# Four node stages of a graph network with their 25 blocks written out, and one combined weight for three vector axes

## The reference

```python
h = relu(layernorm(x))
# layer 0, before its 103125 edges: two node-wise maps, scaled by the node's number z
s0, s1 = (h_s @ W_sc0) * z / 8, einsum('nuc,uw->nwc', h_v, W_sc1) * z / sqrt(32)
h0, h1 = (h_s @ W_l1_0) * z / 8, einsum('nuc,uw->nwc', h_v, W_l1_1) * z / sqrt(32)
# edges: gather h0, h1 at the source, weight by an MLP of the edge, sum at the target: ns (n,96), nv (n,96,3)
# layer 0's end
x = x + concat(sin * s0 + cos * (ns @ W_l2_0) * z / sqrt(96),
               sin * s1 + cos * einsum('nuc,uw->nwc', nv, W_l2_1) * z / sqrt(96))
# layer 2 needs h with features down the partitions; layer 3 maps the normed h twice, and its sums once
```

## Time and profile before

| | |
|---|---|
| median of 3 runs | 11916.89 us (11911.71 to 11928.06) |
| profiled execution, its own time | 11895.75 us |
| its span | 11893.6 us |
| TensorE busy | 8785.1 us, 74% |
| VectorE busy | 8795.3 us, 74% |
| GpSimd busy | 7695.5 us, 65% |
| ScalarE busy | 4487.7 us, 38% |

### The profile page before, as it was taken

One profiled execution on the slowest core, in us unless ns is written; L12 is line 12 of the kernel. 1 busy time (PEld: TensorE's weight loads), 2 busy tenths in 40 slices (PEclk: granted clock), 3 DMA queues, 4 the chain that ended last, 5 costly groups with the idle time before them and its releaser, 6 DMA issues. The chain is left out here.

```text
span 11893.6 us, 249543 instructions
## 1 busy us (share of the span) xinstructions
PE 8785.1 (74%) x62786; PEld 6128.9 (52%) x62787; DVE 8795.3 (74%) x26209; ACT 4487.7 (38%) x15002; POOL 7695.5 (65%) x12520
## 2 busy tenths in 40 slices
PE   4655555199995676666677767588888888888887
PEld 2111111067774444444444433277777777777776
DVE  8977777378884444443555569588999889999997
ACT  0000000056662111111222200177767777776775
POOL 1777777657774777772677700077777777777775
PEclk9777777589996888886899989699999999999998
DMA  4111111023332333331333367100000000000000
GB/s 138 28 28 31 28 28 27 13 62 77 77 77 49 76 76 76 76 76 34 91 91 90 85 116 140 24 22 21 22 21 21 21 21 21 21 22 21 21 22 21
DMA packets 901065, 597.78 MB, mean 50 GB/s; under 512 B 654029, under 2 KB 831011, under 8 KB 898312
## 3 DMA queue, kind: packets, MB, share of 16 engines
q0 software_dynamic: 235616, 359.73, 12.0%
q1 hardware_dynamic: 650440, 197.82, 9.2%
q10 hardware_dynamic: 14624, 35.51, 0.8%
HBM read 512.98 MB, written 79.56 MB: 50 GB/s over the span
## 5 line engine op out<-in xcount | busy, mean ns | idle before, releaser
L1278 POOL DMA_INDIRECT l1s_node_rows<-node_table,l1s_edge_rows x1216 | 1310.6, 1078 | 467.0 <-issue 366.4
L1624 POOL DMA_INDIRECT l2s_node_rows<-node_table,l2s_edge_rows x864 | 858.1, 993 | 513.9 <-issue 262.7
L557 POOL DMA_INDIRECT rows_by_src<-row_s,pos_i x812 | 788.2, 971 | 467.8 <-issue 467.5
L837 POOL DMA_INDIRECT l_source_rows<-node_table,l_edge_rows x880 | 879.8, 1000 | 291.6 <-issue 208.1
L2307 POOL DMA_INDIRECT l_source_rows<-node_table,l_edge_rows x866 | 854.2, 986 | 300.9 <-issue 192.2
L535 PE MATMUL rank<-onehots_and_before,lower_h 128*128 128x427 f16 x812 | 363.7, 448 | 915.7 <-DVE onehots_and_before L490 852.9
L557 POOL DMA_INDIRECT rows_by_dst<-row_d,pos_i x812 | 787.9, 970 | 267.4 <-issue 267.4
L490 DVE TENSOR_REDUCE onehots_and_before<-onehots_and_before 128x427 f16<-128x2135 f16 x202 | 861.4, 4264 | 0.0
L1389 ACT COPY l1s_outer<-l1s_p_outer 128x1024 f32<-128x1024 f32 x304 | 307.6, 1012 | 1447.9 <-PE l1s_p_outer L1363 1320.1
L1360 PE MATMUL l1s_p_outer<-l1s_edge_by_node,l1s_node_rows 128*64 128x128 f32 x4864 | 402.4, 317 | 608.1 <-DMA l1s_node_rows<-node_table,l1s_edge_rows 593.4
L1309 DVE TENSOR_TENSOR l_sums_s<-l_sums_s,l1s_p_sums_s 128x8 f32 x1280 | 207.3, 162 | 726.7 <-PE l1s_p_sums_v L1343 587.0
(11 more groups left out here) (546 smaller groups left out, 28989.7 us busy)
## 6 DMA issues: line engine op xcount, KB each, us to landing
l_xv_by<-h_turned_l SPq DMA_DIRECT2D x120, 320.0 KB
l_source_rows<-node_table,l_edge_rows POOLq DMA_INDIRECT x1746
l_xs_by<-h_turned_l SPq DMA_DIRECT2D x40, 640.0 KB
l1s_edge_rows<-rows_by_src SPq DMA_DIRECT2D x1216, 19.5 KB
l1s_node_rows<-node_table,l1s_edge_rows POOLq DMA_INDIRECT x1216
rows_by_src<-pad_rows_s ACTq DMA_DIRECT2D x16, 1053.0 KB
l2s_edge_rows<-rows_by_src SPq DMA_DIRECT2D x216, 78.0 KB
l_edge_rows<-rows_by_dst SPq DMA_DIRECT2D x220, 72.0 KB
```

The source lines that it names most:

```text
L557: pool.indirect_dma_start(rows_, bass.IndirectOffsetOnAxis(ap=pos_i[:, k, o, t:t + 1].bitcast(U32), axis=0), tile[:, k, t, :], None).then_ ...
L837: pool.indirect_dma_start(xg[k][:, s, :], None, K["table0"], bass.IndirectOffsetOnAxis(ap=pay[k][:, s, D_SRC:D_SRC + 1].bitcast(U32), axis ...
L1278: pool.indirect_dma_start(xg[q][:, s, :], None, table, bass.IndirectOffsetOnAxis(ap=pay[q][:, s, S_DST:S_DST + 1].bitcast(U32), axis=0)).t ...
L1624: pool.indirect_dma_start(xg[k][:, s, :], None, table, bass.IndirectOffsetOnAxis(ap=pay[k][:, s, S_DST:S_DST + 1].bitcast(U32), axis=0)).t ...
```

## The change

In the three functions the loop over blocks is written out by the program that builds the kernel, with fixed addresses. The copies to a fixed buffer are gone: TensorE turns the rows where they lie. GpSimd does nothing in these stages any more. In `stage_turn` there are two PSUM banks instead of one, and the even blocks are copied out by ScalarE, the odd ones by VectorE. In l0-end the sums are turned in the order in which they lie: scalars (96), dots (96), and the y1 part in pieces of 128 and 64. The weight of the axes becomes three matrices of 128 x 96 with the axes' blocks in their places and zeros elsewhere (`l2_1_by_axis`), and three accumulating matmuls of 128 rows and 96 columns take the place of the three of 96 rows and 32 columns. VectorE clears the two PSUM banks first, since part of what ScalarE copies out is never written. The weight takes 6 loads instead of 1 and a memset.

```diff
 # stage_project (l0p, l3p, l3q)
-                def take(b, k):
-                    pool.wait_ge(turned, b + 1)
...
-                    nc.gpsimd.tensor_copy(hb[k][:, :], H[:, bass.ds(b, 1), :].rearrange("p o f -> p (o f)")).then_inc(taken, 1)
...
                 def turn_block(b, k):
-                    pe.wait_ge(taken, b + 1)
+                    if b >= 2:
+                        pe.wait_ge(copied, b - 1)
+                    nc.tensor.transpose(turn[k][:, 0:P], H[:, b, 0:P], K["ident"][:, :])
+                    nc.tensor.transpose(turn[k][0:D - P, P:2 * P], H[:, b, P:D], K["ident"][:, :]).then_inc(turned, 1)
...
-                with pe.Fori(0, NB // 2) as i:
-                    for k in range(2):
-                        turn_block(2 * i + (k + 1), 1 - k)
-                        project(2 * i + k, k)
-                project(NB - 1, 0)
+                for b in range(NB):
+                    if b + 1 < NB:
+                        turn_block(b + 1, (b + 1) % 2)
+                    project(b, b % 2)
 # stage_layer0: weights
-        l2_0, l2_1 = sb("l2_0", [MS, CS]), sb("l2_1", [MS, CV])
+        l2_0, l2_1 = sb("l2_0", [MS, CS]), sb("l2_1_by_axis", [P, 3, 3 * CV])
...
-                    load(l2_1[:, :], "L0_gnn_W_l2_1")
+                    for i in range(3):
+                        to = slice(i * CV, (i + 1) * CV)
+                        load(l2_1[to, 0, to], "L0_gnn_W_l2_1", slice(CS, MS))
+                        load(l2_1[i % 2 * CS:(i % 2 + 1) * CS, 1 + i // 2, to], "L0_gnn_W_l2_1", slice(0, CS))
...
+                    nc.vector.memset(l2_1[:, :, :], 0.0)
                     nc.vector.memset(fc1[:, :, :], 0.0).then_inc(w_clear, 1)
-                    dve.wait_ge(w_in, 16 * 14)
+                    dve.wait_ge(w_in, 16 * 19)
 # stage_layer0: l0-end
-                        nc.gpsimd.tensor_copy(ab[k][:, 0:MS], of[:, AT_S:AT_Y1])
-                        nc.gpsimd.tensor_copy(vectors[:, :, 0:CS], of[:, AT_Y1:MW].rearrange("p (i c) -> p i c", i=3))
-                        nc.gpsimd.tensor_copy(vectors[:, :, CS:MS], of[:, 0:AT_S].rearrange("p (i c) -> p i c", i=3)).then_inc(taken, 1)
...
+                    for k in range(2):
+                        ins = nc.vector.memset(p_t[k][:, :], 0.0)
+                    ins.then_inc(cleared, 1)
...
-                        for j in range(4):
-                            ins = nc.tensor.transpose(p_t[k][0:MS, j * P:(j + 1) * P], ab[k][:, j * MS:(j + 1) * MS], K["ident"][:, :])
+                        nc.tensor.transpose(p_t[k][0:MS, 0:P], acc[:, b, AT_S:AT_Y1], K["ident"][:, :])
+                        nc.tensor.transpose(p_t[k][0:3 * CV, P:2 * P], acc[:, b, 0:3 * CV], K["ident"][:, :])
+                        nc.tensor.transpose(p_t[k][:, 2 * P:3 * P], acc[:, b, AT_Y1:AT_Y1 + 2 * CS], K["ident"][:, :])
+                        ins = nc.tensor.transpose(p_t[k][0:CS, 3 * P:4 * P], acc[:, b, AT_Y1 + 2 * CS:MW], K["ident"][:, :])
...
-                        for i in range(3):
-                            ins = nc.tensor.matmul(p_o[k][:, CS + CV * i:CS + CV * (i + 1)], at_[k][:, (i + 1) * P:(i + 2) * P], l2_1[:, :], start=True, stop=True)
+                        for n in range(3):
+                            ins = nc.tensor.matmul(p_o[k][:, CS:D], at_[k][:, (n + 1) * P:(n + 2) * P], l2_1[:, n, :], start=n == 0, stop=n == 2)
-                        nc.scalar.copy(at_[k][:, :], p_t[k][0:MS, :]).then_inc(copied, 1)
+                        nc.scalar.copy(at_[b % 2][:, :], p_t[b % 2][:, :]).then_inc(copied, 1)
 # stage_turn (l2t)
-                with dve.Fori(0, NB) as b:
-                    dve.wait_ge(turned, b + 1)
-                    nc.vector.tensor_copy(hb[:, :], H[:, bass.ds(b, 1), :].rearrange("p o f -> p (o f)")).then_inc(taken, 1)
...
+                for b in range(NB):
+                    k = b % 2
+                    if b >= 2:
+                        pe.wait_ge((even_copied, odd_copied)[k], b // 2)
+                    nc.tensor.transpose(turn[k][:, 0:P], H[:, b, 0:P], K["ident"][:, :])
+                    nc.tensor.transpose(turn[k][0:D - P, P:2 * P], H[:, b, P:D], K["ident"][:, :]).then_inc(turned, 1)
...
+                for b in range(0, NB, 2):
+                    act.wait_ge(turned, b + 1)
+                    nc.scalar.copy(ht1[:, b * P:(b + 1) * P], turn[0][:, 0:P])
+                    nc.scalar.copy(ht2[:, b * P:(b + 1) * P], turn[0][0:D - P, P:2 * P]).then_inc(even_copied, 1)
...
+                for b in range(1, NB, 2):
+                    dve.wait_ge(turned, b + 1)
+                    nc.vector.tensor_copy(ht1[:, b * P:(b + 1) * P], turn[1][:, 0:P])
+                    nc.vector.tensor_copy(ht2[:, b * P:(b + 1) * P], turn[1][0:D - P, P:2 * P]).then_inc(odd_copied, 1)
```

More of the change, by code:

```diff
@@ L641, in stage_project @@
[L641 to L646, removed]
-                for k in range(2):
-                    step(2 * i + k, k)
-            step(NB - 1, 0)
-        with nc.Block() as block:
-            @block.gpsimd
-            def _(pool):
-                pool.sem_inc(copied, FREE)
-                def take(b, k):
-                    pool.wait_ge(turned, b + 1)
-                    pool.sem_inc(pool_seen, 1)
-                    nc.gpsimd.tensor_copy(hb[k][:, :], H[:, bass.ds(b, 1), :].rearrange("p o f -> p (o f)")).then_inc(taken, 1)
-                blocks(pool, take)
+        turned, copied, projected, stored = (sem(n) for n in ("turned", "copied", "projected", "stored"))
@@ L983, in stage_layer0 @@
-            FREE = 2
-            def blocks(eng, step):
-                with eng.Fori(0, NB // 2) as i:
-                    for k in range(2):
-                        step(2 * i + k, k)
-                step(NB - 1, 0)
-            with nc.Block() as block:
-                @block.gpsimd
-                def _(pool):
-                    pool.sem_inc(copied, FREE)
-                    def take(b, k):
-                        pool.wait_ge(turned, b + 1)
-                        pool.sem_inc(pool_seen, 1)
-                        of = acc[:, bass.ds(b, 1), :].rearrange("p o f -> p (o f)")
-                        vectors = ab[k][:, MS:MW].rearrange("p (i c) -> p i c", i=3)
-                        nc.gpsimd.tensor_copy(ab[k][:, 0:MS], of[:, AT_S:AT_Y1])
-                        nc.gpsimd.tensor_copy(vectors[:, :, 0:CS], of[:, AT_Y1:MW].rearrange("p (i c) -> p i c", i=3))
-                        nc.gpsimd.tensor_copy(vectors[:, :, CS:MS], of[:, 0:AT_S].rearrange("p (i c) -> p i c", i=3)).then_inc(taken, 1)
-                    blocks(pool, take)
+            cleared, turned, copied, mapped, x_done = (semi(n) for n in ("cleared", "turned", "copied", "mapped", "x_done"))
@@ L1036, in map_block @@
+                        if b >= 2:
+                            pe.wait_ge(x_done, b - 1)
+                        nc.tensor.matmul(p_o[k][:, 0:CS], at_[k][0:MS, 0:P], l2_0[:, :], start=True, stop=True)
+                        for n in range(3):
+                            ins = nc.tensor.matmul(p_o[k][:, CS:D], at_[k][:, (n + 1) * P:(n + 2) * P], l2_1[:, n, :], start=n == 0, stop=n == 2)
                         ins.then_inc(mapped, 1)
+                    pe.wait_ge(cleared, 1)
                     turn_block(0, 0)
-                    with pe.Fori(0, NB // 2) as i:
-                        for k in range(2):
-                            turn_block(2 * i + (k + 1), 1 - k)
-                            map_block(2 * i + k, k)
@@ L1044, in _ @@
-                    map_block(NB - 1, 0)
+                    for b in range(NB):
+                        if b + 1 < NB:
+                            turn_block(b + 1, (b + 1) % 2)
+                        map_block(b, b % 2)
                 @block.scalar
                 def _(act):
-                    def copy(b, k):
-                        act.wait_ge(turned, b + (1 + FREE))
-                        act.wait_ge(mapped, b + 1)
-                        nc.scalar.copy(at_[k][:, :], p_t[k][0:MS, :]).then_inc(copied, 1)
@@ L1053, in _ @@
-                    blocks(act, copy)
+                    for b in range(NB):
+                        act.wait_ge(turned, b + 1)
+                        if b >= 2:
+                            act.wait_ge(mapped, b - 1)
+                        nc.scalar.copy(at_[b % 2][:, :], p_t[b % 2][:, :]).then_inc(copied, 1)
 def stage_finish(nc, A, K, out):
```

88 lines of the change are left out of this document (31 added, 57 removed).

## The result

The changed kernel takes **11869.18 us** (median of 6 runs, 11865.42 to 11870.82), the kernel before, run beside it, 11916.18 us (6 runs, 11911.71 to 11928.06): **-47.0 us**, ratio 0.9959, 95% interval 0.9946 to 0.9972. That is less than before by more than the 0.2% that a measurement can tell.

A forecast was written before the change was run, and what follows sets the result against it. No engine was busy over 74%; stages follow at barriers, so each gains what its ending engine loses. -15.2 - 1.8 + 2.7 - 21.5 = -35.8 us, from 11916.9 to 11881 us; range 11862 to 11912, the forecast's own 11869 to 11895.

The forecast's parts named there:

- l0-end, -21.5 forecast: Layer 0's end stage: the clock rises, 2.5 blocks at 2.56 us and 22.5 at 1.45, with memsets -21.5 us.
- Twelve records at l2a's 0.124 us are 1.49; I take 1.45 us per block: l0-end after the clock rises: twelve TensorE records per block at stage l2a's spacing, taken as 1.45 us per block.
- The 0.13 us for the change of width at the low clock: l0-end: going from 128 to 64 stationary columns adds 0.13 us per block, 2.43 becoming 2.56 us.
- 6.5 was taken: l0-end: the clock rises after 6.5 us, later than in l2a; the stage was judged nearer to l2a than l1u.
- The rule of busy time: Skill's claim that the clock follows TensorE's busy time; by it l0-end had nothing to win and the sum was -14.1 us.
- l2t, -15.2 forecast: Stage l2t: two banks' round trips overlap, 1.44 us for two blocks, 33.7 us becoming 18.5.
- ScalarE's bank keeps its 1.35 us: l2t: the round trip of ScalarE's bank stays 1.35 us, now for two blocks.
- the bound of 12 us: l2t's better bound: if only TensorE's records counted, 0.45 us per block, the stage takes 12 us, -21 us.
- Projects, -1.8 forecast: l0p, l3p, l3q: GpSimd's first copy and loop set-up go, 0.6 us each; bounds -0.4 and -0.9 each.
- The third rival: GpSimd's copy bounds the projects: 75 blocks would save 35 us more, 11846 us; chance 0.05.
- Weights, +2.7 forecast: Layer 0's weights before l0p: five more loads 2.3 us, memset 0.3, scaling 0.1; bounds +1.5 and +3.5.
- Straight-line code slower to supply: Rival: the written-out blocks' instructions are slower to supply than a loop's; 11943 us at 0.5 us per block; chance 0.05.

The follow-up runs named there:

- e3: Kernel after, l0-end's three last matmuls per block moving 32 columns instead of 96, into columns of their own: stage 63.38 us, ratio 0.9988.
- e4: Kernel before, loop and GpSimd's copies kept, l0-end's weights laid out over 96 columns: stage 51.64 us, ratio 0.9985.
- e8: Kernel after with e6, e7, four banks in l2t and l1u's last matmul padded to 128 rows: ratio 0.9868.
- e9: Same program as e8, on another chip: 11699.36 us against 11900.37 for the kernel before, ratio 0.9829.
- e2: Kernel before with l2t written out, rows turned where they lie, one bank, both copies on ScalarE: stage 30.02 us, ratio 1.0.
- e12: Kernel after with both of l2t's banks copied by ScalarE, VectorE idle: stage 15.74 us.
- e5: Kernel before with only the three new project stages (written out, no GpSimd copies): l0p, l3p, l3q 77.79, 77.67 and 50.78 us.
- e6: Kernel after, second matmul of l0p, l3p, l3q padded with zeros from 32 to 128 rows: stages 36.74, 35.99, 23.76 us; ratio 0.9905.
- e7: Kernel after, layer 0's last weights loaded behind the bins' load, cleared by GpSimd, scaled after l0p: weights' block 13.14 us (17.66).
- e11: Kernel before, loops and GpSimd's copies kept, only the second matmul of l0p, l3p, l3q padded to 128 rows: 11795.21 us, ratio 0.9911.
- e1: Kernel before with the new l2t alone (written out, two banks, ScalarE and VectorE): stage 15.81 us, kernel 11884.02 us, ratio 0.9986.

## Why the prediction was right, and where its sizes were off

The direction and the mechanism held: the time came from l0-end's clock and l2t's second bank, the projects gave little, the weights cost a little. The forecast's 11881 us was 12 us too high, though within the range; 11869.18 is the very end of the forecast's own 11869 to 11895. The stages' share of the 12 us is 7.2, all of it more gain than was forecast, in these terms:

- **l0-end, -21.5 forecast, -25.3 measured.** "Twelve records at l2a's 0.124 us are 1.49; I take 1.45 us per block" was the mis-sized term. 0.124 is a mean over l2a, whose records stand 0.109 us apart but for two places in a block where it goes over to other widths, which cost some 0.15 us each. What came here is 12 x 0.109 = 1.31: L975 to L978 start 0.11 us apart, and neither the change to 64 stationary columns nor 96 moving ones added anything. Over 22.5 blocks that is 3.2 us. The 0.13 us for the change of width at the low clock was not there either (2.44, not 2.56), and the clock rose 5.9 us after the first transpose where 6.5 was taken, which the same stage in other executions (5.9 to 9.0) does not tell apart.
- **l0-end, the reason for the rise.** The prediction judged it by moved columns and rows, against l2a and l1u. e3 shows the columns: same code, same busy time, 32 in place of 96, and 0.50 throughout. e4 shows that loop and copies don't forbid it. That the rise came so early was in part luck: 6.5 us was a judgement between l2a and l1u, and e4, with the same 96 columns, rose after 34.7 us and gained 11.6 us in place of 25.3. The comparison with l1u ("a fifth of its records hold 33 rows") is borne out by e8 and e9: full rows there, and it rises.
- **The rule of busy time.** The Trainium skill (TensorE: Matmul & The Clock Gate, Part 1) ties the clock to how busy TensorE has been. Measured against it: 60.00 of 60 us busy at 0.50 in e3, 28.90 of 28.9 us busy at 1.00 in the kernel after. By that rule l0-end would have gained nothing; it gained 25.3 us. What the page says of rests agrees: each of the changed stages starts at 0.50 in the profiles of before and after, behind 14 to 215 us without a matmul.
- **l2t, -15.2 forecast, -18.2 measured.** "ScalarE's bank keeps its 1.35 us" failed. Written out, that trip is 1.19 us (e2), VectorE's 1.25, so 12 x (1.44 - 1.25) = 2.3 us; 0.6 us more is the start, where the first transpose comes 0.16 us behind the barrier in place of 0.74 (VectorE's copy of the first row and the loop's set-up stood there). Of the reason, "since both copiers and both banks are separate", only the banks count: one copier does as well (e12). And the bound of 12 us, "if only TensorE's records counted", took the low clock for granted; with four banks and the clock up the stage takes 8.5 us (e9).
- **Projects, -1.8 forecast, -2.8 measured.** 0.96, 0.92 and 0.95 us, against 0.6 taken: a little beyond the bound of 0.9. Step 3.05 as said. The third rival is out: e5 has no copy and the same lengths, and e6 shows what 0.43 of the 0.46 us were.
- **Weights, +2.7 forecast, +3.3 measured.** The bins' load moved by 3.1 us instead of 2.6: the six loads of 32-column pieces take 3.23 / 6 = 0.54 us each, not 0.46. They were on the path, as e7 shows.
- **Straight-line code slower to supply:** no such stall. l0p's steps are 3.05 us in both forms, l0-end's high-clock block 1.31 written out and 1.30 in the loop (e4).
- **Base.** Summing against the profiled execution and quoting against the median was right: of the 21 us by which before's profiled execution lay under the median, its edge loops of layers 2 and 3 can be 15.

What the change was is then clear from the experiments. Its visible part, 25 blocks written out and GpSimd's copies gone, brought 2.8 us in the projects, 4.3 in l2t and nothing in l0-end. The second bank brought 14 us, and moving 96 columns of a weight padded with zeros, in place of 32, 25 us.

## What to carry to other kernels

Read the granted clock of each short TensorE stage, not its busy share: a stage at 100% and 0.50 may have a factor of two in it. Padding rows or columns with zeros cost nothing here at the low clock (a block of 2.44 us with 96 columns against 2.43 with 32; 2.62 with 128 rows against 3.05 with 32), and it brought the high one (e6, e11: 110 and 105 us for a few memsets). Where a stage is a round trip through PSUM, add a bank before adding an engine (e12), and try whether more banks take out TensorE's pauses (e9: four here).

## What the runs showed that I had not expected

- 32 rows in one matmul of each block cost l0p more than half of its time: 3.05 us against 1.29 with 128 rows, of which 0.43 us is the change of rows itself and the rest the clock.
- Between e3 (never rises in 60 us), e4 (after 34.7 us) and the kernel after (5.9 us) there is no sharp line between stages that rise and stages that don't. The moment also moves between executions of one and the same stage (l0-end 5.9 to 9.0 us, the stage 38.0 to 39.5; l2t with two banks after 14.0 us in e1 and not at all in others), so a stage this short can't be forecast to better than a microsecond or two.
- On one chip (e5's profile) the sort took 3050 us in place of 2162 and layer 1's edge loop 2379 in place of 1743, with l0p and l3q the same as in the kernel after and l2t as before to 0.1 us. Comparisons hold within a chip, or stage by stage.
